# Attention scores of a graph network: every fourth pair's left product gathered instead of multiplied, destination one-hots from spread rows, loop unrolled

## The chip, the cores and the metric

One core of one Trainium2 chip runs the whole program. The metric is device time in microseconds of one execution, as a median over runs. The core has the engines TensorE (PE; its weight loads are listed as PEld), VectorE (DVE), ScalarE (ACT), GpSimd (POOL) and SyncE (SP), which work in parallel and wait for one another on semaphores, and 16 DMA engines.

## The reference, cut to what matters

Four graph layers run one after another over 3125 nodes with 128 features (D) and 50000 edges sorted by destination: a relational layer, a GCN layer with batch norm, a GATv2 layer with 4 heads (H), and two transformer convolutions. The change lies in the scores of the GATv2 layer (its self loops are handled apart, in `gat_nodes`):

```python
xl = (x @ W_l + b_l).reshape(N, H, C)              # left product, C = 128
xr = (x @ W_r + b_r).reshape(N, H, C)              # right product
e = leaky_relu(xl[src] + xr[dst], 0.2)
alpha = einsum('ehc,hc->eh', e, att)               # one score for each edge and head
```

The kernel splits leaky_relu(z) into 0.2 z + 0.8 max(z, 0): the linear part comes from two small products kept for each node (`lin`), the rest ("kink") from max(z, 0) * att summed over the 128 columns of a head.

## The kernel before, in words

The edges lie in 416 "pairs": a pair is 128 edge slots, all with destinations in one window of 125 nodes (there are 25 windows). A group is G = 4 pairs, so there are 104 groups. Up to `gat_scores` the path is: `gcn_sums` sums the GCN messages, `batch_norm` ends with SP writing the normed x into `x_table` in DRAM (L1216, 125 partitions x 25 windows x 512 bytes), `gat_nodes` computes for each of the 25 windows the left product (PE, L1302) and the right product (L1303), adds them on DVE for the self scores (L1355, L1357, L1362), and splits the right product into three bf16 parts `m.xr3` with ACT and POOL (L1311, L1314, L1324, L1328). Each of these functions is a block of its own, and a block begins only when all engines have left the one before.

`gat_scores` (from L1370) works on a group like this. POOL issues four indirect DMAs (L992), each of which gathers 128 rows of 132 floats of `x_table` by source; 8 groups of buffers (slots) are in flight. SP writes the gathered rows of a group to `x_rows` in DRAM for a later function (L1013). DVE compares the destinations with 0..124 to make one-hots `hot` with edges on partitions (L1002), two groups ahead. PE transposes the four gathered tiles (fp32, L1461) and the four one-hots (bf16, L1463); ACT copies both to SBUF (L1443, L1444). For each pair PE then accumulates z = x[src] @ W_l + xr[dst] in a PSUM bank: the fp32 product with W_l (L1477, two matmul records of 512 columns), the small linear part (L1478) and three bf16 one-hot products (L1481). DVE reads z with one SCALAR_TENSOR_TENSOR for each head (L1423, four for a pair, 16 for a group), whose sum over the columns is the kink. After the four pairs it adds the linear parts to the scores with small instructions (L1428, L1431, L1433) and has copied the source's part before (L1416).

The order is a hand-written one. Each of the four z banks belongs to one pair of the group (j), so the product of pair j of a group waits for `z_read`, DVE's reading of pair j of the group before: PE can be at most one group ahead of DVE. The turn of group g+1 stands ahead of the products of group g on PE. PE, DVE and SP run loops whose body is 8 groups long, so 13 rounds of it; POOL's gathers are unrolled. The later functions `conv_layer` (two of them) are wholly unrolled and build one-hots otherwise: SP spreads a row of destinations over 125 partitions by a DMA (L1797), and DVE compares it with each partition's own number (L1834), which needs no transposes. They gather rows of 256 floats (L1778).

Of the kernel before, what the change touches and what calls it, by code (L numbers as in the profile page):

```python
# [16 lines left out]
ENG = mybir.EngineType  # L17
# [4 lines left out]
P = 128  # L22
# [69 lines left out]
def chunk_view(flat, c):  # L92

    return flat[:, H * CHUNK_AT[c]:H * (CHUNK_AT[c] + CHUNK[c])].rearrange("l (h p) -> l h p", h=H)

# [910 lines left out]
def put_aside(nc, block, loop, aside, kept_rows, first):  # L1006

    @block.sync
    def _(sp):
        with sp.Fori(0, loop.steps) as i:  # L1010
            for b in range(loop.slots):
                sp.wait_ge(loop.come[b], 64 * i + 64)
                sp.dma_start(kept_rows[bass.ds(loop.slots * i + b, 1), :, :].rearrange("a l (j d) -> (a l) j d", j=G),  # L1013
                             loop.got[:, b, :, first:first + D]).then_inc(aside[b], 16)
        for b in range(loop.slots):
            sp.wait_ge(aside[b], 16 * loop.steps)


# [171 lines left out]
def batch_norm(nc, m, ins, x_table):  # L1190

    with ExitStack() as ctx:
# [12 lines left out]
        def _(sp):  # L1205
# [11 lines left out]
            sp.wait_ge(stored, 16)  # L1217
# [46 lines left out]
def gat_nodes(nc, m, ins, x_table):  # L1264
# [3 lines left out]
    with ExitStack() as ctx:  # L1268
# [11 lines left out]
            "t3", "c3", "lr_done", "z_ready", "scored", "w_lin_ready", "lin_done", "lin_ready", "chain3", "stored3"))  # L1280
        part0, part1, part2, less0, xr_ready = sem("part0"), sem("part1"), sem("part2"), sem("less0"), sem("xr_ready")
        block = ctx.enter_context(nc.Block())

        @block.sync
        def _(sp):
            sp.wait_ge(lin_ready, 1)
            sp.dma_start(nodes(x_table)[:, :, D:D + H], lin[:, :, 0, :]).then_inc(stored, 16)
            sp.wait_ge(stored, 16)

        @block.tensor  # L1290
        def _(pe):
# [7 lines left out]
            for w in range(W):  # L1299
                if w >= 2:  # L1300
                    pe.wait_ge(zed, w - 1)
                nc.tensor.matmul(lb[w % 2][0:Q, :], xt[:, w, :], m.gat_wl[:, :], start=True, stop=True)  # L1302
                nc.tensor.matmul(rb[w % 2][0:Q, :], xt[:, w, :], wr[:, :], start=True, stop=True).then_inc(done, 1)  # L1303

        @block.scalar
        def _(act):
            turn_windows_act(nc, act, m, xt, tb, turned, copied)
            for w in range(W + 1):
                if w < W:
                    act.wait_ge(xr_ready, w + 1)  # L1310
                    nc.scalar.copy(m.xr3[:, w, 0, :], rest[:, w % 3, :]).then_inc(part0, 1)  # L1311
# [20 lines left out]
        def _(dve):  # L1332
# [18 lines left out]
            for w in range(W):  # L1351
# [5 lines left out]
                v.tensor_tensor(z[:, w % 2, :], lb[w % 2][0:Q, :], rest[:, w % 3, :], ALU.add).then_inc(zed, 1)  # L1357
# [12 lines left out]
def gat_scores(nc, m, x_table, x_rows):  # L1370

    with ExitStack() as ctx:
        sb, sem, bank = scope(nc, ctx)
        loop = PairLoop(nc, m, ctx, x_table, width=D + H, hot_dt=BF16)
        got, hot = loop.got, loop.hot
        got_t, hot_t = sb("got_t", [P, 2, G, P]), sb("hot_t", [Q, 2, G, P], BF16)
        junk = sb("junk", [P, G, H, D])
        score, src_lin = sb("score", [P, 2, G, H]), sb("src_lin", [P, 2, G, H])  # L1380
        got_b, hot_b = bank("got_b"), bank("hot_b", (P, 1024), BF16)
        z = [bank(f"z{j}") for j in range(G)]
        lin = [bank(f"lin{b}", (P, G, 3, H)) for b in range(2)]
        turned, copied_t, z_done, z_read, lin_kept, summed, out = (sem(n) for n in (
            "turned", "copied_t", "z_done", "z_read", "lin_kept", "summed", "alpha_out"))
        aside = [sem(f"aside{b}") for b in range(8)]
        block = ctx.enter_context(nc.Block())


        put_aside(nc, block, loop, aside, x_rows, 0)  # L1390

        @block.gpsimd
        def _(pool):
            def wait_free(g, slot):
                pool.wait_ge(turned, g + 1)
                pool.wait_ge(lin_kept, g + 1)
                pool.wait_ge(aside[slot], 16 * (g // loop.slots) + 16)

            loop.gathers(pool, wait_free, PAIRS // G + 1)

        @block.vector
        def _(dve):
            v = nc.vector
            dve.sem_inc(z_read, G)
            dve.sem_inc(out, 2)
            for b in range(2):
                loop.one_hots(b * G, b)
            for c in range(len(CHUNK)):
                wide = loop.slots * G
                with dve.Fori(0, CHUNK[c] // wide) as i0:  # L1410
                    i = i0 + CHUNK_AT[c] // wide
                    for slot in range(loop.slots):
                        g, at, b = loop.slots * i + slot, i * (loop.slots * G) + slot * G, slot % 2
                        here = i0 * (loop.slots * G) + slot * G
                        dve.wait_ge(loop.come[slot], 64 * i + 64)
                        v.tensor_copy(src_lin[:, b, :, :], got[:, slot, :, D:D + H]).then_inc(lin_kept, 1)  # L1416
                        dve.wait_ge(turned, g + 1)
                        loop.one_hots(at + 2 * G, b)
                        for j in range(G):
                            dve.wait_ge(z_done, 4 * g + (j + 1))  # L1420
                            dve.wait_ge(z_read, 4 * g + (j + 1))
                            for h in range(H):
                                last = v.scalar_tensor_tensor(junk[:, j, h, :], z[j][:, h * D:(h + 1) * D], 0.0,  # L1423
# [728 lines left out]
```

## Time and profile before

| | us |
|---|---|
| median of 3 runs | 5079.29 |
| lowest, highest | 5068.19, 5083.59 |
| the profiled execution: its own time | 5059.56 |
| its span, first to last instruction | 5057.7 |
| `gat_nodes`, first to last instruction, about | 1823 to 1948 |
| `gat_scores`, about | 1949 to 2758 |

Times within the trace count from the start of the span. The profile's groups of instructions give busy time, the mean of one, and the idle time of the engine ahead of them with what ended it. "Issue" is time in which nothing that the profile shows was waited for, "remote" an event whose author it cannot name. Matmuls are pipelined, so their durations overlap; the distance between their starts tells more.

### The profile page before, as it was taken

To read this page: it belongs to the slowest core of one execution; us is meant where nothing else is said; L and a number is where in the kernel's file an instruction comes from. 1 tells how busy PE (TensorE), PEld (TensorE's weight loads), DVE (VectorE), ACT (ScalarE), POOL (GpSimd) and SP (SyncE) were. 2 spreads that over 40 slices of the span, in tenths; PEclk is the share of its full clock that TensorE was granted. 3 is DMA by queue.
4 is the path that set the end of the run, shared out by engine and by line. 5 is a ranking of instruction groups with operands and counts; after the bars stand their busy time and mean duration, and the time that the engine had idled before them with its cause. 6 is when DMAs were issued, how large, how long until landed. Compare 5 with 4: busy or idle time off the path is not lost. (4 is left out here: it accounts for less than half of the span.)

```text
span 5057.7 us, 60146 instructions
## 1 busy us (share of the span) xinstructions
PE 3005.5 (59%) x13959; PEld 1996.8 (39%) x13960; DVE 2647.5 (52%) x8593; ACT 852.1 (17%) x2090; POOL 2458.4 (49%) x2775
## 2 busy tenths in 40 slices
PE   7934555562232345999998799752455663354653
PEld 3413444452222322444444344432344552343653
DVE  8935433361011375665666888852445562353655
ACT  4810000000000011111111677610010110010110
POOL 0051467606676425454553688316555514656540
PEclk9955555565555667999999899875565676565766
DMA  1110111211111101222221122025565643556661
GB/s 61 51 51 14 33 51 50 49 22 47 46 47 47 39 13 49 72 76 70 71 73 34 54 68 68 29 60 149 143 190 160 183 120 111 157 163 174 185 172 52
DMA packets 354155, 417.94 MB, mean 83 GB/s; under 512 B 50799, under 2 KB 263439, under 8 KB 353924
## 3 DMA queue, kind: packets, MB, share of 16 engines
q0 software_dynamic: 80000, 192.10, 15.2%
q1 hardware_dynamic: 273924, 223.21, 14.8%
q8 instruction: 91, 1.49, 0.1%
q14 instruction: 140, 1.15, 0.1%
HBM read 309.07 MB, written 106.05 MB: 82 GB/s over the span
## 5 line engine op out<-in xcount | busy, mean ns | idle before, releaser
L1778 POOL DMA_INDIRECT got<-kv_table,pair_src x832 | 816.2, 981 | 883.8 <-POOLq L57 323.9
L591 POOL DMA_INDIRECT y_got<-y_table,y_idx x416 | 419.6, 1009 | 587.4 <-POOLq L57 278.1
L1989 PE MATMUL psum<-acc 125*128 x1664 | 378.0, 398 | 526.1 <-DVE h L1841 456.5
L992 POOL DMA_INDIRECT got<-x_table,pair_src x420 | 398.0, 948 | 367.3 <-issue 351.1
L1989 PEld LDWEIGHTS psum<-acc 125*128 125x128 f32 x1664 | 327.0, 292 | 576.8 <-issue 574.5
L992 POOL DMA_INDIRECT got<-t_table,pair_src x416 | 406.7, 978 | 300.9 <-issue 121.3
L1423 DVE SCALAR_TENSOR_TENSOR junk<-z,att 128x128 f32<-128x128 f32 x1664 | 369.1, 286 | 245.7 <-PE z L1481 156.5
L1477 PE MATMUL z<-gat_wl,got_t 128*128 128x512 f32 x832 | 442.1, 613 | 54.6 <-DVE junk L1423 35.7
L2001 PE MATMUL psum<-h,acc 128*128 128x128 f32 x1664 | 373.4, 368 | 152.2 <-ACT hot_b L1965 92.5
L1841 DVE TENSOR_TENSOR h<-psum,got 128x512 f32<-128x512 f32 x208 | 143.5, 690 | 573.5 <-remote 217.4
L1182 PE MATMUL sums<-msg,hot 128*125 128x512 f32 x832 | 405.3, 636 | 29.3 <-POOL msg L1123 29.3
L1065 PE MATMUL sums<-got,hot 128*125 128x128 f32 x832 | 173.6, 385 | 418.5 <-DVE hot L1002 315.4
L1002 DVE TENSOR_TENSOR hot<-pair_dst,iota 128x500 f32<-128x500 f32 (+1 forms) x212 | 143.5, 682 | 530.5 <-remote 384.1
L2001 PEld LDWEIGHTS psum<-h,acc 128*128 128x128 f32 x1664 | 317.7, 236 | 194.2 <-issue 170.1
L1481 PE MATMUL z<-xr,hot_t 125*128 x1248 | 340.7, 381 | 0.2 <-issue 0.2
L1065 PEld LDWEIGHTS sums<-got,hot 128*125 128x125 f32 x832 | 155.7, 285 | 437.0 <-issue 436.7
L1168 DVE TENSOR_TENSOR acc<-acc,sums 125x536 f32 x416 | 295.4, 710 | 53.2 <-PE sums L1186 8.3
L738 DVE SCALAR_TENSOR_TENSOR hot_w<-iota,src_loc,psum 128x125 f32<-128x125 f32 x416 | 115.3, 340 | 305.6 <-remote 260.2
L1123 POOL TENSOR_TENSOR msg<-rows,wts 128x512 f32<-128x512 f32 x208 | 246.2, 1203 | 37.4 <-DVE wts L1152 34.4
L1140 ACT ACTIVATE msg<-rows,wts 128x128 f32<-128x128 f32 x832 | 254.1, 388 | 1.5 <-DMA rows<-x_rows 1.5
L1866 DVE TENSOR_TENSOR acc<-pair_row,iota 128x512 f32<-128x512 f32 x208 | 143.6, 690 | 159.6 <-PE psum L2002 67.4
L1965 ACT CAST hot_b<-acc 128x512 bf16<-128x512 f32 x208 | 128.6, 618 | 513.4 <-DVE acc L1866 415.8
(483 smaller groups left out, 5203.9 us busy)
## 6 DMA issues: line engine op xcount, KB each, us to landing
v_rows<-got SPq DMA_DIRECT2D x208, 256.0 KB
small<-v_rows SPq DMA_DIRECT2D x208, 256.0 KB
x_rows<-got SPq DMA_DIRECT2D x104, 256.0 KB
rows<-x_rows SPq DMA_DIRECT2D x104, 256.0 KB, 2.6
dst_row<-dst_rows SPq DMA_DIRECT2D x208, 125.0 KB
got<-kv_table,pair_src POOLq DMA_INDIRECT x832
y_table<-y_stage SPq DMA_DIRECT2D x25, 500.0 KB
got<-x_table,pair_src POOLq DMA_INDIRECT x420
```

The costliest lines, as they stand in the source:

```text
L591: pool.indirect_dma_start(out=got[:, slot, j, :], out_offset=None, in_=y_table[:, :], in_offset=bass.IndirectOffsetOnAxis(ap=m.y_idx[:, co ...
L992: pool.indirect_dma_start(out=self.got[:, slot, j, :], out_offset=None, in_=self.table[:, :], in_offset=bass.IndirectOffsetOnAxis(ap=self. ...
L1065: last = t.matmul(sums[0:Q, bass.ds(ws[j] * D, D)], loop.hot[:, b, j, :], loop.got[:, slot, j, :], start=False, stop=False)
L1140: last = nc.scalar.activation(msg[:, b, j, h * D:(h + 1) * D], rows[:, b, j, :], ACT.Copy, scale=wts[:, b, j, h:h + 1])
L1168: v.tensor_tensor(row, row, sums[j][0:Q, 0:H * D + 6 * H], ALU.add).then_inc(read, 1)
L1182: t.matmul(sums[j][0:Q, 0:H * D], hot[:, b, j, :], msg[:, b, j, :], start=True, stop=True)
L1423: last = v.scalar_tensor_tensor(junk[:, j, h, :], z[j][:, h * D:(h + 1) * D], 0.0, m.att[:, h * D:(h + 1) * D], ALU.max, ALU.mult, accum_o ...
L1477: t.matmul(z[j][:, :], got_t[:, b, j, :], m.gat_wl[:, :], start=True, stop=False)
L1481: last = t.matmul(z[j][:, :], hot_t[:, b, j, :], m.xr3[:, bass.ds(ws[j], 1), k, :].rearrange("q o d -> q (o d)"), start=False, stop=(k == 2))
L1778: pool.indirect_dma_start(out=got[:, slot, j, :], out_offset=None, in_=kv_table[:, :], in_offset=bass.IndirectOffsetOnAxis(ap=m.pair_src[: ...
L1989: last = t.matmul(work[:, j * P:(j + 1) * P], hot_t[:, g % 2, j // 2, j % 2, :], m.acc[:, bass.ds(ws[j], 1), 0:D].rearrange("q o d -> q (o ...
L2001: t.matmul(psum[:, bass.ds(ws[j] * D, D)], hot[:, s % 2, j // 2, j % 2, :], msg[:, s % 2, j, :], start=False, stop=False)
```

## The change

`batch_norm` and `gat_nodes` write a second table in DRAM, `wide_table`, with a row of 644 floats for each node: x (128), the linear part (4) and the left product x @ W_l (512). For that ACT copies each window's left product from PSUM to SBUF (`left`, three buffers), SP stores it, and DVE's self scores read the copy. In `gat_scores`, pairs 0 to 2 of a group are done as before; pair 3 (`few`) gathers its row of 644 floats from `wide_table`, PE makes only its right product, and one DVE TENSOR_TENSOR adds the gathered left product to it (into `whole`, in SBUF), from which the four head instructions read. The one-hots come from spread rows for all pairs. Slots go from 8 to 6, the store to `x_rows` is two DMAs for a group, the small score instructions run once for two groups, the four loops are unrolled.

```diff
@@ batch_norm
             sp.dma_start(nodes(x_table)[:, :, 0:D], m.x[:, :, :]).then_inc(stored, 16)
-            sp.wait_ge(stored, 16)
+            sp.dma_start(nodes(wide_table)[:, :, 0:D], m.x[:, :, :]).then_inc(stored, 16)
+            sp.wait_ge(stored, 32)
@@ gat_nodes, SP
+            for w in range(W):
+                sp.wait_ge(left_kept, w + 1)
+                sp.dma_start(wide_table[w * Q:(w + 1) * Q, D + H:D + H + H * D], left[:, w % 3, :]).then_inc(left_stored[w % 3], 16)
@@ gat_nodes, PE
-                    pe.wait_ge(zed, w - 1)
+                    pe.wait_ge(left_kept, w - 1)
+                    pe.wait_ge(xr_ready, w - 1)
@@ gat_nodes, ACT
+                    act.wait_ge(done, w + 1)
+                    if w >= 3:
+                        act.wait_ge(left_stored[w % 3], 16 * (w // 3))
+                        act.wait_ge(zed, w - 2)
+                    nc.scalar.copy(left[:, w % 3, :], lb[w % 2][0:Q, :]).then_inc(left_kept, 1)
@@ gat_nodes, DVE
-                v.tensor_tensor(z[:, w % 2, :], lb[w % 2][0:Q, :], rest[:, w % 3, :], ALU.add).then_inc(zed, 1)
+                dve.wait_ge(left_kept, w + 1)
+                v.tensor_tensor(z[:, w % 2, :], left[:, w % 3, :], rest[:, w % 3, :], ALU.add).then_inc(zed, 1)
@@ gat_scores: the new queues (the old ones, in the listing above, go)
         def _(pool):
+            for g in range(groups):
+                slot = g % slots
+                if g >= slots:
+                    pool.wait_ge(turned, g - slots + 1)
+                    pool.wait_ge(scored, (g - slots) // 2 + 1)
+                    pool.wait_ge(aside[slot], 32 * (g // slots))
+                ... (three gathers from x_table into got, one from wide_table into got_w)
         def _(sp):
+            def spread(g):
+                if g >= 3:
+                    sp.wait_ge(hot_ready, g - 2)
+                sp.dma_start(dst_row[:, g % 3, :], row_bc(dst_rows[g, :], Q)).then_inc(row_in[g % 3], 16)
+            for g in range(groups):
+                sp.wait_ge(come[slot], 16 * G * (g // slots + 1))
+                sp.dma_start(kept[:, 0:few, :], got[:, slot, :, 0:D]).then_inc(aside[slot], 16)
+                sp.dma_start(kept[:, few, :], got_w[:, slot, 0:D]).then_inc(aside[slot], 16)
+                if g + 3 < groups:
+                    spread(g + 3)
         def _(dve):
+            def turn_hot(g):
+                dve.wait_ge(row_in[g % 3], 16 * (g // 3 + 1))
+                v.tensor_scalar(hot_t[:, g % 3, :, :].rearrange("q j l -> q (j l)"), dst_row[:, g % 3, :], m.lane[0:Q, :], None,
+                                ALU.is_equal).then_inc(hot_ready, 1)
+            def finish(n):
+                ...
+                v.reduce_sum(part, lin[b][:, :, :, :, :].rearrange("p g j k h -> p h (g j) k"), AX).then_inc(lin_read, 1)
+                dve.wait_ge(z_read, 8 * n + 8)
+                v.tensor_tensor(mine[:, :, 0:few, :], mine[:, :, 0:few, :], got[:, slot:slot + 2, :, D:D + H], ALU.add)
+                v.tensor_tensor(mine[:, :, few, :], mine[:, :, few, :], got_w[:, slot:slot + 2, D:D + H], ALU.add).then_inc(scored, 1)
+                dve.wait_ge(scored, n + 1)
+                dve.wait_ge(lin_read, n + 1)
+                v.tensor_tensor(part, part, mine.rearrange("p g j h -> p h (g j)"), ALU.add).then_inc(out, 1)
+            for g in range(groups):
+                if g + 2 < groups:
+                    turn_hot(g + 2)
+                dve.wait_ge(z_done, 4 * g + 1)
+                dve.wait_ge(come[g % slots], 16 * G * (g // slots + 1))
+                if g >= 2:
+                    dve.wait_ge(z_read, 4 * g - 4)
+                v.tensor_tensor(sum_of, z[few][:, :], got_w[:, g % slots, D + H:D + H + H * D], ALU.add).then_inc(added, 1)
+                for j in range(few):
+                    dve.wait_ge(z_done, 4 * g + j + 2)
+                    if g:
+                        dve.wait_ge(z_read, 4 * g)
+                    kinks(g, j, z[j]).then_inc(z_read, 1)
+                dve.wait_ge(added, g + 1)
+                kinks(g, few, sum_of).then_inc(z_read, 1)
+                if b:
+                    finish(g // 2)
         def _(act):
+            for g in range(groups):
+                act.wait_ge(turned, g + 1)
+                if g >= 2:
+                    act.wait_ge(z_done, 4 * g - 4)
+                nc.scalar.copy(got_t[:, g % 2, :, :].rearrange("p j e -> p (j e)"), got_b[:, 0:few * P]).then_inc(copied, 1)
         def _(pe):
+            def of_node(g, j, w, first):      # the small linear part and three bf16 one-hot products
+                ...
+            for g in range(groups):
+                ws = windows(nc, m.pair_win_i, ENG.PE, g * G, G)
+                if g + 1 < groups:
+                    turn(g + 1)               # three fp32 transposes; waits for come and copied
+                pe.wait_ge(hot_ready, g + 1)
+                if g:
+                    pe.wait_ge(added, g)
+                if g % 2 == 0 and g >= 4:
+                    pe.wait_ge(lin_read, g // 2 - 1)
+                of_node(g, few, ws[few], True)
+                pe.wait_ge(copied, g + 1)
+                for j in range(few):
+                    if g:
+                        pe.wait_ge(z_read, 4 * g - 3 + j)
+                    t.matmul(z[j][:, :], got_t[:, g % 2, j, :], m.gat_wl[:, :], start=True, stop=False)
+                    of_node(g, j, ws[j], False)
```

## Rows read from the trace of the kernel before

**Rows 1.** Stages of `gat_scores`: us, engine busy (instructions), clock, DMA share, GB/s

```profile
core 0: us, PE busy (x) PEld busy (x) DVE busy (x) ACT busy (x) POOL busy (x), PEclk, DMA share, GB/s
1950.00:2019.00 69.00, 34.58 (x126) 16.67 (x127) 16.88 (x125) 5.37 (x10) 42.77 (x46) 0.66 0.34 86
2240.00:2288.00 48.00, 48.00 (x225) 24.20 (x224) 32.64 (x253) 7.52 (x14) 26.06 (x28) 1.00 0.29 73
2288.00:2700.00 412.00, 388.36 (x1771) 192.12 (x1770) 257.95 (x2053) 59.05 (x110) 209.98 (x222) 0.99 0.28 72
```

**Rows 2.** The same stretches, the matmuls of line 1477 alone (8 for a group)

```profile
1950.00:2019.00 69.00, 19.58 (x30) 6.46 (x30) 0.66 0.34 86
2288.00:2700.00 412.00, 232.97 (x443) 79.28 (x443) 0.99 0.28 72
```

**Rows 3.** PE through one undisturbed group: start, duration, instruction, [idle before]

```profile
2243.84 0.60 PE L1461 MATMUL got_b<-ident,got 128*128 128x128 f32 x4
2244.28 0.39 PE L1463 MATMUL hot_b<-ident_b,hot 128*125 128x128 bf16 x4
2244.51 1.08 PE L1477 MATMUL z<-gat_wl,got_t 128*128 128x512 f32 x2
...
2247.64 1.02 PE L1477 MATMUL z<-gat_wl,got_t 128*128 128x512 f32 x2
2248.50 0.17 PE L1478 MATMUL lin<-lin,hot_t 125*128 x1
...
2250.70 0.60 PE L1461 MATMUL got_b<-ident,got 128*128 128x128 f32 x4
```

**Rows 4.** POOL's gathers, 1960 to 2757: count, busy us, mean ns, idle before

```profile
L992 POOL DMA_INDIRECT got<-x_table,pair_src x412 | 390.3, 947 | 362.6 <-issue 349.0 <-PE hot_b L1463 11.6 <-remote 2.0
```

**Rows 5.** DVE at the turn of a loop round, and the stalls behind it

```profile
2289.56 0.17 DVE L1416 COPY src_lin<-got 128x16 f32<-128x16 f32 x1 [2.99 <-issue]
2290.41 0.28 DVE L1423 SCALAR_TENSOR_TENSOR junk<-z,att 128x128 f32<-128x128 f32 x1
2293.78 0.20 DVE L1428 TENSOR_REDUCE alpha<-lin 128x48 f32 x1
...
2323.80 0.29 DVE L1423 SCALAR_TENSOR_TENSOR junk<-z,att 128x128 f32<-128x128 f32 x1 [6.57 <-remote]
```

**Rows 6.** PE around that last stall

```profile
2320.23 0.81 PE L1481 MATMUL z<-xr,hot_t 125*128 x3
2324.95 0.95 PE L1461 MATMUL got_b<-ident,got 128*128 128x128 f32 x4 [3.91 <-ACT hot_t L1444]
```

**Rows 7.** The unrolled `conv_layer` without messages, 3420 to 3600, groups of instructions

```profile
L1778 POOL DMA_INDIRECT got<-kv_table,pair_src x124 | 117.8, 950 | 64.1 <-issue 36.0 <-DVE h L1841 28.1
L1841 DVE TENSOR_TENSOR h<-psum,got 128x512 f32<-128x512 f32 x26 | 18.0, 692 | 135.6 <-DMA dst_rows<-dst_t 96.9 <-issue 32.5 <-PE psum L1989 6.2
L1834 DVE TENSOR_SCALAR acc<-dst_row,lane 125x512 f32<-125x512 bf16 x26 | 12.4, 477 | 0.0
```

**Rows 8.** The same function, 3440 to 3600, columns as in rows 1

```profile
3440.00:3600.00 160.00, 51.78 (x200) 44.52 (x200) 44.29 (x75) 0.00 (x0) 101.11 (x108) 0.50 0.53 149
```

**Rows 9.** POOL's gathers in `gcn_sums`, in order of time

```profile
1441.86 1.38 POOL L992 DMA_INDIRECT got<-t_table,pair_src  x1 [5.00 <-remote]
```

**Rows 10.** DVE in the second `conv_layer` and after, 3700 to 4500, groups of instructions

```profile
L1870 DVE TENSOR_TENSOR h<-small,wts 128x512 f32<-128x512 f32 x97 | 66.5, 686 | 0.0
```

**Rows 11.** From `batch_norm` to `gat_nodes`; the DMA rate from 1800 to 1824

```profile
1801.80 0.28 SPq L1216 DMA_DIRECT2D x_table<-x_nodes  x1
1823.09 1.54 PEld L260 LDWEIGHTS g_t<-ident,x_nodes 125*128 125x128 f32 x8 [51.23 <-issue]
...
GB/s 0 0 0 0 60 101 90 92 85 85 85 86 86 85 84 85 85 85 84 85 85 85 85 86 86 84 84 85 85 85 85 86 86 85 84 19 0 0 0 0
```

**Rows 12.** The window loop of `gat_nodes`, 1845 to 1945, groups of instructions

```profile
L1362 DVE SCALAR_TENSOR_TENSOR junk<-z_self,att 125x128 f32<-125x128 f32 x98 | 69.2, 758 | 0.8
L1311 ACT CAST xr<-rest 125x512 bf16<-125x512 f32 x24 | 14.8, 618 | 73.0 <-DVE rest L1355 73.0
```

More of the change, by code:

```diff
@@ L1367, in _, with gat_scores @@
             v.tensor_tensor(m.self_score[:, :, :], m.self_score[:, :, :], kink[:, :, :], ALU.add)
[L1370 removed]
+def gat_scores(nc, m, x_table, wide_table, dst_rows, x_rows):
     with ExitStack() as ctx:
         sb, sem, bank = scope(nc, ctx)
[L1376 to L1381, printed above, removed]
[L1382 to L1386 removed]
+        groups, few, slots = PAIRS // G, G - 1, 6
+        got, got_w = sb("got", [P, slots, few, D + H]), sb("got_w", [P, slots, D + H + H * D])
+        dst_row, hot_t = sb("dst_row", [Q, 3, G * P], BF16), sb("hot_t", [Q, 3, G, P], BF16)
+        got_t, whole = sb("got_t", [P, 2, few, P]), sb("whole", [P, 2, H, D])
+        score = sb("score", [P, 2, 2, G, H])
+        junk = m.small[:, :, :].rearrange("l p k -> l (p k)")[:, 0:G * H * D].rearrange("l (j h d) -> l j h d", j=G, h=H)
+        got_b = bank("got_b")
+        z = [bank(f"z{j}") for j in range(G)]
+        lin = [bank(f"lin{b}", (P, 2, G, 3, H)) for b in range(2)]
+        hot_ready, turned, copied, z_done, z_read, added, lin_read, scored, out = (sem(n) for n in (
+            "hot_ready", "turned", "copied", "z_done", "z_read", "added", "lin_read", "scored", "alpha_out"))
+        aside = [sem(f"aside{b}") for b in range(slots)]
+        row_in = [sem(f"row_in{i}") for i in range(3)]
+        come = m.come.pop()
@@ L1387, in gat_scores @@
         block = ctx.enter_context(nc.Block())
-        put_aside(nc, block, loop, aside, x_rows, 0)
         @block.gpsimd
         def _(pool):
[L1394 to L1399, printed above, removed]
+            for g in range(groups):
[4 more added lines that the diff above has]
+                    pool.wait_ge(aside[slot], 32 * (g // slots))
+                for j in range(G):
+                    col = g * G + j
+                    at = bass.IndirectOffsetOnAxis(ap=m.pair_src[:, col:col + 1], axis=0)
+                    if j < few:
+                        pool.indirect_dma_start(out=got[:, slot, j, :], out_offset=None, in_=x_table[:, :], in_offset=at
+                                                ).then_inc(come[slot], 16)
+                    else:
+                        pool.indirect_dma_start(out=got_w[:, slot, :], out_offset=None, in_=wide_table[:, :], in_offset=at
+                                                ).then_inc(come[slot], 16)
```

137 lines of the change are left out of this document (52 added, 85 removed).

## The prediction, made before the changed kernel ran

> **What bounds the kernel now.** I read the page first (spans, the 40 slices), then cut the stages by time. In `gat_scores` TensorE sets the pace: from 2288 to 2700 PE is busy 388 of 412 us at a clock of 0.99, from 2240 to 2288 for all of it [rows 1]. The count of the products with W_l, eight for a group, gives the pitch: 443 records in 412 us are 55.4 groups of 7.44 us; 30 records in the first 69 us are 3.75 groups, at a clock of 0.66 while PE still waited [rows 1, 2]. The other 100.25 groups take 738 us (to 2757), 7.36 each. PE's timeline of one undisturbed group shows the floor, 6.86 us from 2243.84 to 2250.70. It splits into 0.44 for the four fp32 transposes, 0.23 for the four one-hot transposes and 6.19 for four pairs; in a pair, the distance from the fp32 product to what follows is 0.86 (2247.64 to 2248.50) [rows 3]. So 0.50 us per group lies above the floor. Part of it shows as stalls: DVE has "issue" for 2.99 us where a round of the loop begins, and it begins the fourth pair's heads at 2323.80 after 6.57 us of "remote" [rows 5], although PE's last matmul of that pair had been due to end at 2321.04; PE then waits 3.91 us for ACT's copies [rows 6]. DVE is busy 258 us in 55.4 groups, 4.66 each [rows 1], so it has slack of 2.2 against PE's floor, and that slack absorbs most such events.
>
> **PE, the term that matters.** Per group the change takes away one fp32 product (0.86), one of the four fp32 transposes (0.44 / 4 = 0.11) and the one-hot transposes (0.23) [rows 3]; no matmul is added. The floor becomes 6.86 − 1.20 = 5.66 us. I keep the old excess of 0.50, because causes of both signs meet there (below): 6.16. Over 100.25 groups that is 618 us against 738: −120. The first groups were held by POOL's first gathers and a slow clock; for 3.75 groups I take 0.8 us each, −3 (0 to −5).
>
> **DVE.** The 16 head instructions of a group take 3.37 us, from 2290.41 to 2293.78 [rows 5], as before. Added is the sum of z and the gathered product. The same operation of the same size, PSUM and SBUF in, takes 0.69 in `conv_layer`; the comparison with the spread row takes 0.48 there, with fp32 out [rows 7]; here it writes bf16, and I take 0.48 with 0.24 as the lower end. The small instructions come to about 0.5 per group (an estimate from 0.20 for the reduction and 0.17 for a small copy [rows 5], now five for two groups, with their waits). Sum: 3.37 + 0.69 + 0.48 + 0.50 = 5.04. This is beside PE's 5.66 while nothing is late; the slack falls from 2.2 to 0.6 us. The reading of `whole` makes four head instructions have two SBUF inputs. Beside POOL's elementwise work such an instruction took 0.758 instead of 0.211 [rows 12, 5], which for four would be +2.2; beside gathers a two-SBUF-input instruction of 512 columns took 0.686, no more than the PSUM one [rows 10, 7]. POOL only gathers here, so I take 0 of 0 to 2.2.
>
> **POOL.** A gather takes 0.95 us and about 0.30 of issue in front of it [rows 4, 9]: 1.25, so 5.0 for a group, under 5.66. A row of 2576 bytes instead of 528 changes POOL's part little if a row of 1024 bytes is a guide: 0.950 against 0.947 [rows 7, 4]. It does grow where it falls on a DVE instruction with two SBUF inputs: 1.38 at 1441.86 [rows 9]. With all four so it is 1.7 × 4 = 6.7 at the worst; with one or two so, 5.4 to 5.9. I take 5.4, hidden. The wait for `aside` with six slots instead of eight asks for stores two groups or so earlier; at 6.16 a group six slots are 37 us, and gathers land within a few.
> The Trainium skill speaks against the change here ("SBUF — State Buffer", Who interferes with whom): VectorE's second pair of SBUF ports is GpSimd's only one, an exclusive lock, and descriptors of a gather can't be written meanwhile. By this rule the one-input comparison in bf16 and the four heads read from `whole` hold up gathers; the row at 1441.86 agrees in size. By it, with all four gathers of a group at 1.7 us, the pitch would be 6.7.
>
> **DMA.** Per group: three gathers of 68 KB, one of 330 KB, 262 KB to `x_rows`, 128 KB of spread rows: 923 KB. At 6.16 us that is 150 GB/s. `conv_layer` ran at 149 GB/s with a DMA share of 0.53, with 108 gathers in 160 us, 5.93 us a group [rows 8]; before, this stage ran at 72 at a share of 0.28 [rows 1]. So transfers fit, with twice the share and later landings. Cost 0, and 0.5 per group as the other end.
>
> **Excess.** For less: no taken branches for PE, DVE and SP, so the 2.99 of "issue" every eighth group goes (0.37 per group if it was wholly on the path, which it isn't). For more: DVE's slack is a quarter of what it was, so a lateness like the 6.57 reaches PE more often. The unrolled `conv_layer` is not free of it: DVE idles 135.6 us of 180 with waits put down to a DMA that had long ended [rows 7]. I keep 0.50, ends 0 and 2.2.
>
> **`batch_norm`.** SP's store of `x_table` is issued at 1801.80, the rate is about 85 GB/s until 1821, and the next function begins at 1823.09: nothing else runs. The store is 1.6 MB, 18.8 us at that rate [rows 11]. The second store, of the same size in packets of 512 bytes, is behind it and waited for: +19 (0 if it found idle DMA engines, +25 if the wider stride slows it).
> The rate, a third of what the DMA engines move at full share in rows 1 (72 / 0.28 = 257), suggests few engines in use. The Trainium skill ("DMA: Bandwidth & Descriptors", Why a DMA increments its semaphore by 16 and not by 1) has it so: a copy uses the largest number up to 16 that divides the outer dimension, and the lowest-numbered engines; 125 gives 5, and the second store the same 5. By it the +19 stands and 0 is excluded.
>
> **`gat_nodes`.** DVE sets the pace here, 98 head instructions with 0.8 us of idle time in 100 us; ACT has 73 us idle in the same stretch, so one more copy per window of about 0.62 is hidden [rows 12], and so is the store of 256 KB per window (3.0 us at 85 GB/s, of 4.1). DVE's sum now reads two SBUF tiles and the first window waits for ACT: +1 (0 to +5, the last store included). Waits queued behind: the copy stands in ACT's order ahead of the casts, and PE's next left product waits for it.
>
> **Sum.** −120 − 3 + 19 + 1 = −103. The profiled execution has a span of 5057.7 and its own time is 5059.56: 4957. It lies 19.7 below the median of the runs, 5079.29; on the median's basis the forecast is 4976.
>
> **The rivals,** all on the median's basis.
> *Floor reached.* If the excess came from loop turns and the old coupling, the pitch is 5.66: 567 − 738 = −171, −154 in all, 4925. For it: 2.99 of "issue" [rows 5]. Against: the 6.57 comes in the middle of a round. Partly so gives 4925 to 4950. The Trainium skill ("Runtime: NRT & Kernel Launch", Instruction fetch mechanics) says that a taken branch breaks the sequential prefetch and costs a fetch; by it this case would be the one. Chance 0.25.
> *POOL or the transfers bound it.* Pitch 6.6 to 7.1 from the worst POOL row and the DMA end: −76 to −26 with the scores, −59 to −9 in all: 5020 to 5070. For it: 5.4 is only 0.3 below the floor. Against: 5.93 in `conv_layer`, whose gathers are of this kind [rows 8]. Chance 0.18.
> *DVE sets the pace, slower.* In 2288 to 2700 DVE idled 7.44 − 4.66 = 2.78 per group. If that is not PE's slowness but late signals that no faster PE brings forward, the new pitch is 5.04 + 2.78 = 7.82: 784 − 738 = +46, +63 in all: 5142. The point from which this decides is a pitch of 7.19. For it: the stalls of rows 5 and 6, in which DVE and not PE was behind. Against: 48 us with PE busy throughout, where DVE idled and nobody was late [rows 1]. Chance 0.12.
> *The scores don't get shorter in time because the clock falls:* PE waiting more, it could sink from 0.99 toward 0.50 as in `conv_layer`, where PE was busy a third of the time [rows 8, 1]. At 5.66 of 6.16 PE stays above 0.9 busy. It goes with the last two rivals and has no chance of its own.
>
> **How the numbers follow.** The likeliest, 6.0 to 6.5 per group, 4960 to 5010, has 0.45; the others 0.25, 0.18, 0.12. From no change this measurement tells 0.3%, 15 us. Faster: 0.45 + 0.25 + most of the third (0.13) = 0.83; same 0.05; slower 0.12. The range holds 8 in 10 from 4905 (floor reached and the second store cheaper) to 5080.
>
> **What would show it.** In the changed profile: pitch from the count of W_l records (six for a group); the distance between turns in an undisturbed group should be 5.66; DVE busy about 5.0 per group with 0.7 for the sum; a gather of `wide_table` near 0.95; some 38 us between the first store of x and `gat_nodes`; `gat_nodes` at 4.1 per window. It is wrong if PE's busy share in `gat_scores` falls below 0.85, if gathers have a mean above 1.2, or if DVE's waits on "remote" grow.

## The result, and the profile after

| | us |
|---|---|
| kernel before, median of 5 runs | 5079.29 |
| changed kernel, median of 5 runs (5098.45 to 5113.10) | 5106.12 |
| ratio, 95% interval | 1.0062 (1.0039 to 1.0085) |
| forecast, its range | 4976 (4905 to 5080) |
| profiled execution: own time, span | 5106.12, 5104.4 |

One execution of the kernel before took 7606.9 us; it counts in the median, which leaves a gap of 27 us, and not in the ratio. So it became slower by about 0.6% where I had forecast 103 us less. On a chip measured later (e5) the same changed kernel was faster than the kernel before by 107 us, on another (e1 to e3) its variants were faster by 102 to 108, and on two more the conditions of the first came back. Most of what follows is about that difference.

PE did get its shorter group. This is PE's timeline of a group of the changed kernel that nothing disturbs (start, duration, instruction); [rows 3] show the same for before:

```profile
2308.26 0.49 PE L1505 MATMUL got_b<-ident,got 128*128 128x128 f32 x3
2309.27 1.02 PE L1532 MATMUL z<-gat_wl,got_t 128*128 128x512 f32 x2
2310.13 0.17 PE L1510 MATMUL lin<-lin,hot_t 125*128 x1
...
2313.87 0.49 PE L1505 MATMUL got_b<-ident,got 128*128 128x128 f32 x3
```

From turn to turn it is 5.61 us, where I had worked out 5.66, against 6.86 before. But the stage didn't follow. Two rows of the stretch from 2100 to 2700, all instructions and then line 1532 (the product with W_l) alone, columns as in [rows 1]:

```profile
2100.00:2700.00 600.00, 484.25 (x1950) 223.46 (x1950) 368.11 (x2807) 37.77 (x79) 295.06 (x312) 0.94 0.47 121
```

```profile
2100.00:2700.00 600.00, 263.36 (x468) 91.43 (x468) 0.94 0.47 121
```

468 records, six for a group, are 78 groups in 600 us: 7.69 us each, 2.1 above the undisturbed group, where before it was 7.44 and 0.6 above [rows 1 to 3]. PE is busy 81% of the time, not 94%. DVE's busy time is 368.11 / 78 = 4.72 per group and POOL's gathers 295.06 / 78 = 3.78, so neither is full. The groups of instructions from 1985 to 2802 show that the parts cost what was forecast (count, busy, mean ns, idle before them):

```profile
L1409 POOL DMA_INDIRECT got<-x_table,pair_src x312 | 294.9, 945 | 366.1 <-issue 360.5 <-POOLq L57 2.8 <-PE got_b L1505 2.7
L1448 DVE SCALAR_TENSOR_TENSOR small<-z,att 128x128 f32<-128x128 f32 x1248 | 281.2, 287 | 281.5 <-remote 151.0 <-PE z L1513 98.6 <-issue 31.7
L1412 POOL DMA_INDIRECT got_w<-wide_table,pair_src x104 | 98.4, 946 | 31.7 <-issue 31.7
L1448 DVE SCALAR_TENSOR_TENSOR small<-whole,att 128x128 f32<-128x128 f32 x416 | 96.5, 287 | 0.9 <-issue 0.9
L1477 DVE TENSOR_TENSOR whole<-z,got_w 128x512 f32<-128x512 f32 x104 | 71.1, 683 | 14.4 <-issue 10.5 <-PE z L1513 3.7
L1494 ACT COPY got_t<-got_b 128x384 f32<-128x384 f32 x104 | 49.7, 478 | 759.0 <-remote 441.8 <-PE got_b L1505 168.7 <-issue 142.1
L1443 DVE TENSOR_SCALAR hot_t<-dst_row,lane 125x512 bf16<-125x512 bf16 x104 | 38.1, 366 | 7.3 <-DMA dst_row<-dst_rows 6.8 <-issue 0.5
```

The wide gather takes 0.946 us, like the narrow one, the sum 0.683, the comparison 0.366, and the heads that read `whole` 287 ns like those that read PSUM. What is large is idle time that ends on "remote": 151.0 us for DVE and 441.8 for ACT. One such stop in the timeline, from 2300 to 2335:

```profile
2314.23 0.81 PE L1513 MATMUL z<-xr,hot_t 125*128 x3
2316.78 0.29 DVE L1448 SCALAR_TENSOR_TENSOR small<-z,att 128x128 f32<-128x128 f32 x1 [5.67 <-remote]
2317.00 0.48 ACT L1494 COPY got_t<-got_b 128x384 f32<-128x384 f32 x1 [7.73 <-remote]
...
2317.83 0.30 PEld L1532 LDWEIGHTS z<-gat_wl,got_t 128*128 128x128 f32 x2 [3.29 <-ACT got_t L1494]
2317.86 1.09 PE L1532 MATMUL z<-gat_wl,got_t 128*128 128x512 f32 x2 [2.83 <-DVE small L1448]
...
2321.33 0.94 POOL L1409 DMA_INDIRECT got<-x_table,pair_src  x1 [6.27 <-issue]
```

PE has finished its pairs and transposes, yet DVE and ACT wait for PE, and go on within 0.22 us of each other. It is the picture of [rows 5, 6], about once in every two groups: from 2020 to 2790 DVE has 46 gaps of over 1.5 us, together 196 us. Before there were hardly fewer, 49 with 165 us from 2020 to 2750. What changed is how much of that reaches PE. The whole stage, before and then after, columns as in [rows 1]:

```profile
1947.50:2758.20 810.70, 737.80 (x3336) 365.21 (x3336) 487.87 (x3850) 112.73 (x210) 398.01 (x420) 0.96 0.27 69
1983.10:2802.10 819.00, 648.25 (x2600) 299.48 (x2600) 491.27 (x3745) 49.73 (x104) 393.33 (x416) 0.93 0.46 118
```

PE's busy time fell by 90 us, but its idle time rose by 98, from 72.9 to 170.8 us.

### When the signals were posted

The trace also holds the time of each update of a semaphore. I set it against the end of the instruction that makes the update. Around this stop:

```
 ends     posted   by
 2309.27  -        ACT   copied          (POOL begins the fifth gather of a run at 2310.37)
 2310.51  2311.08  DVE   hot_ready
 2311.11  2311.77  DVE   added
 2310.96  2316.76  PE    z_done, pair 0
 2312.50  2316.84  PE    z_done, pair 1
 2314.03  2316.92  PE    z_done, pair 2  (POOL's last gather of the run ends at 2315.06)
 2314.36  2316.97  PE    turned
 2315.03  2317.03  PE    z_done, fourth pair of the next group
 2317.47  2317.48  ACT   copied
 2320.25  2320.27  DVE   z_read
```

From 2311.77 to 2316.76 no update is posted, then five come within 0.27 us; pair 0's is 5.8 us behind its instruction. DVE starts 0.02 us after pair 0's update, so the record tells the time at which DVE could go on. While POOL rests an update comes 0.01 us behind its instruction. So I sorted all updates of PE, DVE and ACT by the number of gathers that POOL had issued back to back when the instruction ended (a run ends with a pause of 0.5 us). Delay, mean us, and share above 1 us, `gat_scores`:

| gathers in the run | before: n, mean, share | changed: n, mean, share |
|---|---|---|
| none | 484, 0.06, 0.00 | 460, 0.02, 0.00 |
| 1 | 163, 0.23, 0.05 | 119, 0.01, 0.00 |
| 2 | 142, 0.28, 0.06 | 91, 0.01, 0.00 |
| 3 | 162, 0.70, 0.19 | 10, 0.40, 0.20 |
| 4 | 161, 1.04, 0.37 | 138, 1.48, 0.69 |
| 5 | 21, 4.20, 0.76 | 81, 3.48, 0.72 |
| 6 | 16, 4.67, 1.00 | 81, 4.08, 0.94 |
| 7 and 8 | 43, 2.26, 0.81 | 97, 2.72, 0.98 |

Where an update has no record of its own, the delay is counted from the latest instruction that it can belong to, so these are lower bounds. In the kernel before 80 of 1192 updates fell on the fifth gather of a run or later (7%), in the changed one 259 of 1077 (24%). The reason stands in POOL's queue: `pool.wait_ge(scored, (g - slots) // 2 + 1)`, with `scored` raised once for two groups, gives leave for eight gathers at once. 45 of the changed kernel's runs are 8 long; before, 61 were 4 long and 14 were 8.

### The profile page after: what moved, and what is told of

It reads as the page before. It is cut to its first block and busy times, and to the rows that moved or that the text cites. A ratio compares the mean times of both kernels' runs of the same rounds, so it can differ in the third digit from the quotient of the medians.

```text
span 5104.4 us, 56905 instructions
## 1 busy us (share of the span) xinstructions
PE 2912.2 (57%) x13211; PEld 1927.1 (38%) x13224; DVE 2651.1 (52%) x8487; ACT 801.4 (16%) x2009; POOL 2456.9 (48%) x2771
## 5 line engine op out<-in xcount | busy, mean ns | idle before, releaser
L1409 POOL DMA_INDIRECT got<-x_table,pair_src x312 | 294.9, 945 | 366.1 <-issue 360.5
L2045 PE MATMUL psum<-h,acc 128*128 128x128 f32 x1664 | 375.7, 368 | 150.0 <-ACT hot_b L2009 91.8
L1532 PE MATMUL z<-gat_wl,got_t 128*128 128x512 f32 x624 | 352.5, 648 | 143.3 <-remote 69.4
L1448 DVE SCALAR_TENSOR_TENSOR small<-z,att 128x128 f32<-128x128 f32 x1248 | 281.2, 287 | 281.5 <-remote 151.0
L1513 PE MATMUL z<-xr,hot_t 125*128 x1248 | 355.6, 395 | 0.0
L1007 DVE TENSOR_TENSOR hot<-pair_dst,iota 128x500 f32<-128x500 f32 x106 | 71.3, 682 | 531.9 <-remote 375.8
L853 PE MATMUL psum<-y_got,hot_w 128*125 128x128 f32 x832 | 210.2, 429 | 0.2 <-DVE hot_w L743 0.2
```

The source lines that it names most:

```text
L1409: pool.indirect_dma_start(out=got[:, slot, j, :], out_offset=None, in_=x_table[:, :], in_offset=at).then_inc(come[slot], 16)
L1448: last = v.scalar_tensor_tensor(junk[:, j, h, :], zj[:, h * D:(h + 1) * D], 0.0, m.att[:, h * D:(h + 1) * D], ALU.max, ALU.mult, accum_out ...
L1513: last = t.matmul(z[j][:, :], hot, m.xr3[:, bass.ds(w, 1), k, :].rearrange("q o d -> q (o d)"), start=(first and k == 0), stop=(k == 2))
L1532: t.matmul(z[j][:, :], got_t[:, g % 2, j, :], m.gat_wl[:, :], start=True, stop=False)
L2045: t.matmul(psum[:, bass.ds(ws[j] * D, D)], hot[:, s % 2, j // 2, j % 2, :], msg[:, s % 2, j, :], start=False, stop=False)
```

## The experiments

A table first; the stage is from the last instruction of `gat_nodes` to the last of `gat_scores`. Each block (e1 to e4, e5 to e7, e8 and e9, e10 to e12) ran on a chip of its own beside the kernel before, whose stage and late updates are known from the first session alone. e3 and e10 leave out three quarters of the gathers of `gat_scores` and so don't give the right scores.

| kernel | median | before there | ratio (95%) | stage | late updates (> 1 us) |
|---|---|---|---|---|---|
| before | 5079.29 | | | 810.7 | 177 of 1192 |
| changed | 5106.12 | 5079.29 | 1.0062 (1.0039 to 1.0085) | 819.0 | 328 of 1077 |
| e1 leave once a group | 4283.90 | 4391.55 | 0.9751 (0.9720 to 0.9782) | 602.8 | 0 of 1176 |
| e2 two waits a group | 4287.08 | 4391.55 | 0.9761 (0.9730 to 0.9792) | 603.0 | 0 |
| e3 one gather of four | 4289.25 | 4391.55 | 0.9757 (0.9724 to 0.9790) | 603.1 | 0 |
| e4 before, paced | 4400.41 | 4391.55 | 1.0017 (0.9999 to 1.0034) | 730.5 | 0 of 1231 |
| e5 changed | 4297.57 | 4404.77 | 0.9756 (0.9737 to 0.9775) | 602.8 | 0 of 1179 |
| e6 store beside | 4282.10 | 4404.77 | 0.9737 (0.9712 to 0.9762) | 603.2 | 0 |
| e7 all multiplied | 4393.62 | 4404.77 | 0.9976 (0.9964 to 0.9987) | 702.1 | 0 |
| e8 all together | 4923.18 | 5072.30 | 0.9713 (0.9688 to 0.9738) | 690.0 | 223 of 948 |
| e9 split stores | 5031.91 | 5072.30 | 0.9918 (0.9886 to 0.9950) | 783.2 | 274 of 1058 |
| e10 one gather of four | 4894.67 | 5082.42 | 0.9623 (0.9604 to 0.9642) | 613.7 | 0 of 985 |
| e11 before, paced | 5044.55 | 5082.42 | 0.9918 (0.9898 to 0.9937) | 776.3 | 245 of 1138 |
| e12 wait for each gather | 4967.37 | 5082.42 | 0.9767 (0.9748 to 0.9787) | 685.0 | 295 of 843 |

### e1 to e4: waits that shorten POOL's runs, and most gathers left out

```diff
 e1: once, e2: at j 0 and 2, e12: at every j (in the changed kernel)
                 for j in range(G):
+                    if g >= slots and j % every == 0:
+                        pool.wait_ge(z_read, 4 * (g - 4) + j)
 e3, e10 (every wait on `come` lowered to match)
+                    if g >= slots and j:
+                        continue
 e4, e11 (in the kernel before)
+                if g >= self.slots and j == 2:
+                    pool.wait_ge(z_read, G + 4 * (g - self.slots) + j)
```

> The changed kernel with one more wait of POOL: before the four gathers of group g it waits until DVE has read all pairs of group g-5, so it gets leave once a group instead of once for two groups (the wait on `scored`). Theory A (bursts): in the trace of the changed kernel, updates of PE's, DVE's and ACT's semaphores come 0.01 us after the instruction when POOL rests or is in its first three gathers, and 1.5 to 6 us late from the fourth gather of a run on; the runs are 8 long because leave comes every second group. Then runs of 4 instead of 8 give a pitch of 6.2 to 6.8 in gat_scores instead of 7.67: about 4980 to 5020. Rival B (PE's sequencer or its instruction stream stops by itself every two groups) and rival C (the doubled DMA traffic delays everything): no change, 5100 to 5115.

> The changed kernel with two more waits of POOL for each group: before its first and third gather it waits until DVE has read the corresponding pair of group g-4, so that no run is longer than 2 while POOL keeps up. Theory A: hardly any late update, pitch 5.7 to 6.2, about 4930 to 4970 us. Rivals B and C: 5100 to 5115, or slower, since POOL gets less lead.

> The changed kernel with only the first of the four gathers of a group from the seventh group on (the other three pairs work on stale rows; three quarters of the gathers are left out). Theory A: no late updates, PE's floor of 5.4 to 5.7 us per group, 4870 to 4910 us. Rival C (traffic) expects the same here, and differs from A in the two runs with waits. Rival B: pitch stays 7.6, 5100.

> The kernel before with one more wait of POOL in gat_scores: the third gather of a group waits until DVE has read two pairs of the group eight earlier, so runs are 2 long instead of 4 to 8. Theory A: the stalls of the kernel before go, its pitch falls from 7.36 to 6.9: -45 us, about 5030. Rivals B and C: no change, 5080.

All three variants of the changed kernel came out alike, 2.4% faster than the kernel before, and the paced kernel before unchanged. But these runs told nothing for theory A over its rivals, because the chip was another one: the kernel before took 4391 us on it instead of 5079, and not one update in any of the four traces is later than 0.02 us, not even behind eight gathers in a row (e1 has 110 updates in runs of five or more). What POOL's waits do could not be seen where nothing is late.

### e5 to e7: the changed kernel where updates are prompt, and its parts

> The changed kernel as it is. In the four runs before this, engines' semaphore updates came 0.01 to 0.02 us after their instruction however long POOL's runs of gathers were, the kernel before took 4391 us instead of 5079, and gat_scores had 5.78 us per group with one gather out of four as well as with all. Theory A' (late updates are a condition of the chip or the session on which the first two profiles were taken, and only there they took the gain away): where updates are prompt this is as fast as the runs with extra waits, 4275 to 4295 beside 4391, ratio 0.975; where they are late, ratio 1.006. Rival: the waits of POOL made those runs fast; then this is at 4400 to 4420 where the kernel before is at 4391.

It is at 0.9756, so the waits were not what had made e1 and e2 fast. The stretch from 1850 to 2250 of its `gat_scores`, all instructions and line 1532 alone:

```profile
1850.00:2250.00 400.00, 400.00 (x1784) 196.85 (x1783) 337.03 (x2571) 33.95 (x71) 269.63 (x285) 1.00 0.64 166
```

```profile
1850.00:2250.00 400.00, 219.17 (x429) 81.16 (x428) 1.00 0.64 166
```

PE is never idle, 429 / 6 = 71.5 groups make 5.59 us each, at a clock of 1.00, and DMA moves 166 GB/s. The traffic was no obstacle. Stage by stage (first to last instruction of a function) the two kinds of chip differ only where POOL gathers. The kernel before itself was not traced on a prompt chip; its paced form e4, which took as long there, stands for it:

| us | before, late | changed, late | e4, prompt | e5, prompt |
|---|---|---|---|---|
| `relation_layer` (gathers) | 798.8 | 803.3 | 605.7 | 604.7 |
| `gcn_sums` (gathers) | 601.7 | 608.2 | 545.9 | 553.8 |
| `batch_norm` | 90.3 | 111.4 | 92.0 | 110.4 |
| `gat_nodes` | 119.0 | 121.2 | 118.2 | 121.5 |
| stage of `gat_scores` (gathers) | 810.7 | 819.0 | 730.5 | 602.8 |
| `gat_sums` | 412.6 | 411.9 | 412.4 | 411.8 |
| both `conv_layer` (gathers) | 1612.8 | 1616.5 | 1270.1 | 1263.3 |

The differences between the first and the third column in the functions that gather add up to 672 us; the two profiled executions differ by 670. And the lateness is not special to `gat_scores`: in the first trace of the kernel before, 14% of the updates in `relation_layer`, 30% in `gcn_sums` and 9% in `conv_layer` are more than 1 us late, in `gat_nodes` and `gat_sums` at most 0.5%, in e5 at most 0.3% in any of them.

The transfers themselves were as quick: the last landing of a group comes 2.65 us (median) behind the end of its fourth gather in the changed kernel of the first session, 3.04 in e5; 1.58 and 1.61 in the kernel before and e4.

```diff
 e6: moved from batch_norm to the head of SP's queue in gat_nodes; `stored` waited for at its end
-            sp.dma_start(nodes(wide_table)[:, :, 0:D], m.x[:, :, :]).then_inc(stored, 16)
 e7
-        groups, few, slots = PAIRS // G, G - 1, 6
+        groups, few, slots = PAIRS // G, G, 6
-                v.tensor_tensor(sum_of, z[few][:, :], got_w[:, g % slots, D + H:D + H + H * D], ALU.add).then_inc(added, 1)
-                of_node(g, few, ws[few], True)
```

> The changed kernel with the store of x into the wide table issued at the start of gat_nodes and waited for at its end, instead of waited for in batch_norm. If the second store stood wholly on the path: 18 to 19 us less than the changed kernel in the same call. If it only shifts the end of gat_nodes: 0 to -5.

15 us less by the medians. `batch_norm` fell from 110.4 to 91.8, and `gat_nodes`, which now shares the DMA engines with the store, rose from 121.5 to 125.8: −18.6 + 4.3 = −14.3. Most of the store's cost was on the path, and nearly a quarter of what was saved comes back in `gat_nodes`.

> The changed kernel with all four pairs multiplied: no gather of the wide table, no sum on DVE, four fp32 transposes; spread rows, unrolled loops, six slots and the stores of the wide table stay. PE's floor is then 6.86 - 0.23 = 6.63 us per group against 5.66. Where updates are prompt: 104 x 0.9 = +90 us beside the changed kernel, so the gather brings nearly all the gain in gat_scores and spread rows 0.2 us per group. Where updates are late and eat the excess: +20 to +60.

The stage is 99 us longer than with the gather, the median 96. Against e4 (730.5), spread rows, unrolled loops and fewer small instructions together are worth 28 us, where the one-hot transposes alone were reckoned at 0.23 × 104 = 24. That leaves some 4 us for the rest. It is an estimate: no run changes the unrolling alone, and e7 is not quite at its floor (from 2050 to 2450 PE is busy 389.36 of 400 us).

### e8 and e9: a chip with late updates again

```diff
 e9: both stores, e8: the store of x_table (e8 has the edits of e6 and e2 too)
-            sp.dma_start(nodes(x_table)[:, :, 0:D], m.x[:, :, :]).then_inc(stored, 16)
+            sp.dma_start(nodes(x_table)[0:112, :, 0:D], m.x[0:112, :, :]).then_inc(stored, 16)
+            sp.dma_start(nodes(x_table)[112:Q, :, 0:D], m.x[112:Q, :, :]).then_inc(stored, 16)
```

> The changed kernel with the wide store beside gat_nodes, the x_table store split into partitions 0 to 111 and 112 to 124, and POOL's two waits per group of the second run. Where updates are prompt: 15 from the moved store (measured) and some 12 from the split: about 4270 beside 4405, ratio 0.969 to 0.972. Where updates are late (kernel before at 5079): theory A (late updates come from the fourth gather of a run on, so short runs avoid them) expects 4900 to 4960; if run length is not what matters there, 5060 to 5090.

> The changed kernel with both stores of x in batch_norm cut into partitions 0 to 111 and 112 to 124. If the store of 125 partitions runs on 5 of the 16 DMA engines (its rate is 85 GB/s) and 112 = 16 x 7 lets it use 16: each store falls from 19 to some 7 us, -24 us beside the changed kernel; 4270 to 4275 beside 4400. If the rate is the limit of 512-byte packets: no change, 4285 to 4300.

The kernel before stood at 5072 here, and updates were late again, in the same way: in e9 2.7% of 705 updates beside no or up to three gathers in a row, and 87% of the 225 from the fifth gather on. e8 and e9 have the same `gat_scores` but for POOL's two waits: 690.0 against 783.2, −93 us. The time is in the range that theory A gave (4923 in 4900 to 4960), but its picture is only half right. POOL did not run two gathers at a time: e8 has 34 runs of 4 and 35 of 6, e9 45 of 8. And late updates did not go, they became less late. Counted over the whole stage, each from the latest instruction that it can belong to, those over 1 us fell from 252 to 194, those over 3 us from 97 to 10. One stretch of each, 2050 to 2450, e8 first:

```profile
2050.00:2450.00 400.00, 369.24 (x1575) 174.70 (x1575) 298.98 (x2267) 30.13 (x63) 239.52 (x252) 0.98 0.57 147
```

```profile
2050.00:2450.00 400.00, 338.15 (x1358) 154.56 (x1359) 257.80 (x1953) 26.37 (x55) 204.41 (x216) 0.94 0.49 126
```

DMA moves more in e8, 147 GB/s against 126, with fewer and shorter delays, so it is not the traffic (rival C) that holds the updates up.

e8 is the fastest complete version on the chips of this kind, 0.9713; part of that is its stores (`batch_norm` 79.0 us). The split in e9 took 24 us off `batch_norm` (111.4 to 87.2), as expected. The rest of e9's gain I can't explain: its `gat_scores` is the changed kernel's unaltered and took 783.2 us, against 819.0 in the first session. So two late chips can differ by 36 us on the same code, and comparisons from one of them to another are no better than that. Without its 24 us e9 would be at 5056, an estimate of the changed kernel on this chip, and not slower than the kernel before there (5072). That the changed kernel is slower where updates are late rests on the first session alone. SP's queue and the next function, the changed kernel and then e9 (start, duration, instruction; a long SPq entry is SP held up in issuing):

```profile
1816.64 0.28 SPq L1208 DMA_DIRECT2D x_table<-x_nodes  x1
1816.96 15.74 SPq L1209 DMA_DIRECT2D wide_table<-x_nodes  x1
1856.67 1.54 PEld L265 LDWEIGHTS g_t<-ident,x_nodes 125*128 125x128 f32 x8 [69.97 <-issue]
```

```profile
1808.32 0.33 SPq L1208 DMA_DIRECT2D x_table<-x_nodes  x1
1808.69 4.28 SPq L1209 DMA_DIRECT2D x_table<-x_nodes  x1
1813.01 1.08 SPq L1210 DMA_DIRECT2D wide_table<-x_nodes  x1
1814.13 6.42 SPq L1211 DMA_DIRECT2D wide_table<-x_nodes  x1
1825.81 1.54 PEld L265 LDWEIGHTS g_t<-ident,x_nodes 125*128 125x128 f32 x8 [47.43 <-issue]
```

From the first store to the next function it is 40.0 us in the one and 17.5 in the other. The mean busy share of the 16 DMA engines is 0.3 at 85 GB/s while the two whole stores run (5 of 16 is 0.31), and 0.9 or more at 188 to 289 GB/s through most of e9's.
That bears out the rule of the Trainium skill ("DMA: Bandwidth & Descriptors", Why a DMA increments its semaphore by 16 and not by 1) that the largest number up to 16 that divides the outer dimension is used, which sends 125 partitions to 5 DMA engines and 112 to 16. Which engines they were, the trace doesn't tell.

### e10 to e12: one more such chip

> The changed kernel with one gather of four from the seventh group on, as in the third run. Where updates are late (the kernel before near 5075): theory A expects no late update and the same 601 us of gat_scores as where they are prompt, -215 beside the changed kernel: near 4890. If gathers are not the cause of the lateness there, gat_scores stays above 750. Where updates are prompt this repeats the third run (4290).

> The kernel before with POOL's third gather of a group waiting for two pairs, as in the fourth run. Where updates are late: runs of 2 in place of 4 to 8 take away most of its stalls: -30 to -50 beside the kernel before. Where prompt: no change.

> The changed kernel with a wait of POOL before each gather of gat_scores (for one more pair read by DVE). Where updates are late: runs of 1 to 2, fewer late updates than with two waits a group (689 us in gat_scores), 620 to 690; the whole near 4900 to 4960. If longer runs remain because POOL falls behind (5.0 us of gathers in a pitch of 5.7), it is no better than two waits. Where prompt: 4285.

With one gather of four, no update is late (0 of 985) and the stage falls to 613.7, 205 us below the changed kernel of the first session (of which some 36 may be the chip, by e9), close to the 603 of the prompt chips, although the untouched `conv_layer` functions take their late 1615.8 in the same trace. The stretch from 2050 to 2450:

```profile
2050.00:2450.00 400.00, 400.00 (x1784) 196.84 (x1783) 334.96 (x2570) 33.95 (x71) 65.99 (x70) 1.00 0.30 82
```

The same trace holds the opposite case. Before the seventh group nothing is left out, and POOL issues its first 24 gathers in a row, to 2013.49. Behind them DVE and ACT stand still until both are let go at once:

```profile
2012.54 0.95 POOL L1414 DMA_INDIRECT got_w<-wide_table,pair_src  x1 [0.30 <-issue]
2016.56 0.29 DVE L1450 SCALAR_TENSOR_TENSOR small<-z,att 128x128 f32<-128x128 f32 x1 [5.43 <-remote]
2016.62 0.48 ACT L1496 COPY got_t<-got_b 128x384 f32<-128x384 f32 x1 [17.86 <-remote]
```

Six updates of that run are over 2 us late, one of PE's 11.5 us; from 2030 to the end of the stage no update is later than 0.02 us. So it is gathers in long runs that hold the updates up, on this chip, and neither PE, nor its program, nor the unrolled code. Nor is it the traffic: 82 GB/s here without a late update, 72 with them in the kernel before.

The paced kernel before gained 38 us, as expected (its waits cost nothing where updates are prompt, e4). But why is not shown: 59 of its runs are still 4 long, and it has more late updates than the kernel before of the first session, not fewer (245 of 1138 against 177 of 1192). A wait for each gather is no better in the stage than two a group (685.0, on another chip than e8's 690.0), and its late updates are more, 295 of 843. Most of its runs are 3 to 5 gathers long all the same. I take it that POOL falls behind after each late update and its waits are then met at once; e1's single wait was not tried where updates are late.

## Why the prediction was wrong

- **What each part costs: right.** PE's group 5.61 (5.66 forecast), wide gather 0.946, sum 0.683, comparison 0.366 (0.48, 0.24 as the lower end). By the busy time of e5, DVE needs 337.03 / 71.5 = 4.71 per group; I had 5.04.
- **`batch_norm`: right,** +21.1 in the first session, +18.4 on the prompt chips (+19). **`gat_nodes`:** +2.2 and +3.3 (+1).
- **The excess over PE's floor: here it failed.** "I keep the old excess of 0.50" made the pitch 6.16. In the first session the excess became 2.1, so the stage took 8 us more instead of 123 less. PE's idle time, which the forecast had left as it was, rose by 98 us, and its busy time fell by 90 us instead of some 123 (the bullet on the clock). On the prompt chips there is none, in either kernel: the stage falls by 128 (730.5 to 602.8), and with `batch_norm` and `gat_nodes` −106 comes out, against −107.2 measured and −103 forecast. That the sum fits there is partly luck: I took both pitches 0.5 too high. Where 0.50 came from I had not asked. It was not a property of PE or of loops, but went with the updates that fell into long runs of gathers; the change raised their share (80 of 1192 in runs of five and more, 259 of 1077). It also took away slack that had covered such delays: e11, in the old order, has 199 updates over 1 us late and PE idles 9 us from 2030 to 2730; e8, in the new one, has 194 and PE idles 47 us from 2000 to 2630.
- **The first groups: −3 was too little.** In the first 71 us of the stage six groups are done (36 records of line 1532), before 3.75. The other 98 take 748 us, 7.63 each. That start, worth about 17 us (2.25 groups), hid part of the loss. The forecast had no term for it, and no run takes it apart.
- **The rival that came true** is "DVE sets the pace": late signals that no faster PE brings forward, pitch 7.82; measured 7.69, with DVE idle 2.97 per group where I had carried over 2.78. Its total, 5142, was 36 us too high. I had given it 0.12 and had the range end below it. For it stood DVE's and ACT's waits on PE with PE's work done [rows 5, 6]; against it I put 48 us without a stall [rows 1], which were 48 us in which POOL's gathers came four at a time with a pause of 1.6 us or more behind each four (none of the 74 updates from 2240 to 2286 is later than 0.65 us).
- **Floor reached:** its pitch of 5.66 is there where updates are prompt (5.59 in e5), but not for its reason, the taken branches: e5's loops are unrolled and e4's not, and in both PE is busy without a break (400 of 400 us, and 500 of 500 from 1850 to 2350). The 2.99 us of "issue" every eighth group are covered by PE's lead.
- **POOL's port:** gathers hardly grew. The longest of 416 took 1.06 us and the mean is 945 ns; those that overlap a head on `whole` have a mean of 954, those that overlap a comparison 959, the others 944. DVE's comparison and sum took no longer than forecast.
The Trainium skill's rule on the shared ports ("SBUF — State Buffer", Who interferes with whom) had no weight here. For a VectorE instruction with two SBUF inputs it holds against GpSimd instructions that read SBUF, not against those that only write it; I had applied it to the heads without that limit.
- **Clock:** PE's stops had a price that I had set at none. The granted clock is 0.94 where it was 0.99; behind a stop a record of line 1532 takes 1.06 us at the lower level instead of 0.59 (51 of 562 between 2060 and 2780; before, 8 of 754). Those 51 alone come to some 24 us (an estimate, 0.47 each).

## What to carry to other kernels

A stall in which an engine waits for another whose work was long done is a cost of its own: find what it goes with (here the length of POOL's run of gathers, from each update's time against its instruction's end) before an "excess" is carried over to a faster loop. A permission that is raised once for two groups makes bursts of twice the length, and a cheap extra wait can shorten them (from 8 gathers to 4 and 6 in e8, −93 us). And if unchanged stages of a program take 10 to 30% longer on one chip than on another, a change must be judged on both.

## What the runs showed of the hardware

- In three of five sessions (the four later ones were on four different chips; that of the first is not on record) updates of semaphores by PE, DVE and ACT were held up, by up to 6 us within the loop of `gat_scores` and by 11.5 us once behind 24 gathers (e10), mostly when POOL had issued four or more gathers of 128 rows back to back. In the stop shown they were then posted within 0.27 us. In the other two sessions no update of `gat_scores` was later than 0.02 us, behind eight gathers in a row either. The program takes 5079 us in the one case and 4400 in the other, and the difference lies in the functions that gather.
- What makes a chip one or the other stays open; nothing in the traces tells it, and the transfers took the same time on both. Whether it is the number of gathers or the time without a pause is open too: gathers 0.3 us apart were counted as one run, and a pause of 0.5 us or more as its end. With the waits of e11 and e12 updates were late behind runs of three as well. By what means gathers hold up the updates of other engines, no run shows.
- A second DMA of 3125 packets behind a first held SP's queue for 15.74 us at its issue.
